# A fused perceiver layer on one core: own-attention links, shift and first expert's chunks issued in another order

## What is computed

```python
x = x + cross_attention(layernorm(x), ctx)   # 16 heads of 16; softmax over 1601 keys
x = x + own_attention(layernorm(x))          # 16 heads of 16, causal, over the batch's 64 rows
x = x + experts(layernorm(x))                # 8 experts 256->1024->256, gelu, best 2 by router
```

## Time and profile before

| | |
|---|---|
| median of 3 runs | 663.91 us (663.18 to 666.14) |
| profiled execution | 663.55 us, its span 661.7 us |
| TensorE busy | 630.8 us, 95% of the span |
| VectorE busy | 475.3 us, 72% |
| ScalarE busy | 329.4 us, 50% |
| GpSimd busy | 301.9 us, 46% |
| TensorE, 400 to 450 us | 45.26 us busy, granted clock 0.97 |
| TensorE, 450 to 500 us | 45.02 us busy, granted clock 0.93 |
| TensorE, 500 to 600 us | 100.00 us busy, granted clock 1.00 |

### The profile page before, as it was taken

One profiled execution on the slowest core, in us unless ns is written; L12 is line 12 of the kernel. 1 busy time (PEld: TensorE's weight loads), 2 busy tenths in 40 slices (PEclk: granted clock), 3 DMA queues, 4 the chain that ended last, 5 costly groups with the idle time before them and its releaser, 6 DMA issues.

```text
span 661.7 us, 15583 instructions
## 1 busy us (share of the span) xinstructions
PE 630.8 (95%) x6304; PEld 532.8 (81%) x6312; DVE 475.3 (72%) x878; ACT 329.4 (50%) x541; POOL 301.9 (46%) x386
## 2 busy tenths in 40 slices
PE   7989999999989989989998999978989999999997
PEld 4778878868877868877887888757879999999997
DVE  4887757667687678688777868686777666656753
ACT  4355655555554555446555545463654444444421
POOL 2138788897686688678678768200000000000000
PEclk9999999999989999999999999998989999999999
DMA  6311110100010010011110000423003302330000
GB/s 184 134 50 52 28 51 26 51 27 26 27 52 1 27 50 27 26 27 51 27 27 26 2 1 2 152 106 127 1 1 128 128 26 104 127 127 0 0 0 33
DMA packets 13285, 34.11 MB, mean 52 GB/s; under 512 B 1563, under 2 KB 10532, under 8 KB 11044
## 3 DMA queue, kind: packets, MB, share of 16 engines
q1 hardware_dynamic: 13188, 33.19, 15.1%
q0 software_dynamic: 32, 0.01, 0.0%
HBM read 32.67 MB, written 0.52 MB: 50 GB/s over the span
## 4 chain that ended last, share of the span: by engine, by line
PE 74%; DVE 13%; issue 5%; ACT 3%; POOL 3%; DMA 2%; SPq 0%; POOLq 0%; DVEq 0%; ACTq 0%
PE bank L1207 46%; PE bank L1396 8%; PE bank L1216 7%; PE bank L1382 4%; PE bank L1277 3%; POOL prob_sum L490 3%; DVE maxes L923 3%; DVE ctx_lo L474 2%; DMA raw<-in_w 1%; ACT k_hi L626 1%; DVE k_lo L904 1%; PE bank L1332 1%; PE bank L1320 1%; PE bank L1304 1%; DVE prob_sum L490 1%
## 5 line engine op out<-in xcount | busy, mean ns | idle before, releaser
L490 POOL TENSOR_TENSOR prob_sum<-probs,prob_sum 128x256 f32<-128x256 f32 x336 | 270.6, 837 | 71.4 <-ACT probs L739 66.4
L739 ACT ACTIVATE probs<-bank 128x1024 f32<-128x1024 f32 (+1 forms) x104 | 106.6, 1025 | 111.6 <-PE bank L1396 99.2
L923 DVE TENSOR_REDUCE maxes<-bank 128x1 f32<-128x400 f32 (+1 forms) x256 | 129.5, 564 | 20.3 <-PE bank L1277 19.8
L721 ACT ACTIVATE h_raw<-bank,b_sb 128x512 f32<-128x512 f32 (+2 forms) x72 | 46.2, 642 | 106.5 <-PE bank L1207 106.3
L904 DVE SCALAR_TENSOR_TENSOR k_lo<-bank,bias_sb,k_hi 128x400 fp32r<-128x400 f32 (+2 forms) x64 | 40.5, 632 | 48.6 <-ACT k_hi L626 48.6
L1207 PE MATMUL bank<-w_hi,h_hi 128*128 128x256 f32 x256 | 73.6, 288 | 0.8 <-DVE h_lo L1142 0.8
L1207 PE MATMUL bank<-w_lo,h_hi 128*128 128x256 f32 x256 | 72.9, 285 | 0.0
L1207 PE MATMUL bank<-w_hi,h_lo 128*128 128x256 f32 x256 | 72.8, 284 | 0.0
L1216 PE MATMUL bank<-probs,v_sb 128*32 128x128 f32 (+1 forms) x1664 | 68.1, 282 | 1.0 <-ACT probs L739 0.5
L1141 DVE CAST h_hi<-h_raw 128x512 fp32r<-128x512 f32 (+2 forms) x72 | 28.5, 396 | 55.5 <-ACT h_raw L721 54.1
L1207 PE MATMUL bank<-wv_hi,ctx_hi 128*128 128x256 f32 (+1 forms) x208 | 65.3, 314 | 2.6 <-DVE maxes L923 2.4
(11 more groups left out here) (155 smaller groups left out, 1389.8 us busy)
## 6 DMA issues: line engine op xcount, KB each, us to landing
raw<-in_w SPq DMA_DIRECT2D x16, 1024.0 KB, 6.8
ctx_raw<-in_ctx_t SPq DMA_DIRECT2D x16, 400.0 KB, 3.6
ctx_raw<-in_ctx_t SPq DMA_DIRECT2D x8, 402.0 KB, 3.8
ctx_raw<-in_ctx_t SPq DMA_DIRECT2D x8, 399.0 KB, 3.6
w_sb<-in_w_t SPq DMA_DIRECT2D x1, 1280.0 KB
w_raw<-in_w_t SPq DMA_DIRECT2D x2, 256.0 KB, 4.7
result<-x_all SPq DMA_DIRECT2D x4, 128.0 KB, 2.0
x_all<-in_x SPq DMA_DIRECT2D x1, 384.0 KB, 4.1
```

What stands on the lines that cost most here:

```text
L490: ins = engine.tensor_tensor(prob_sum[0:ROWS[k], cols], probs[0:ROWS[k], s % 2, cols], acc[0:ROWS[k]], ALU.add)
L721: nc.scalar.activation(h_raw[:, c % 2, 0:width], bank[:, at, 0:width], ACT.Gelu, bias=b1_sb[:, bass.ds(e, 1), c:c + 1].rearrange("p a b -> ...
L739: nc.scalar.activation(probs[0:ROWS[k], s % 2, :].rearrange("p (g n) -> p g n", g=G), bank[0:ROWS[k], score_bank(b, k):score_bank(b, k) + ...
L923: nc.vector.tensor_reduce(maxes[:, g * PAIRS + j, c:c + 1], src[:, 0:width], AX.X, ALU.max).then_inc(read_dve, 1)
```

## The change

Six edits of order; no operation is added, removed or made larger. The table entries of the chain from t10 to the router move one step forward (gt and b2 stay), the second spreading of the own queries stands right behind the first read of the buffer (before the row maxima of s0), `find_shift` stands behind the last step's maxima instead of at the start of the next step (before the context split that used to come between), and the first expert's chunks 0 and 1 go into banks 4 and 5 and stand around the last weighing, before the last denominators; the other chunks follow one place sooner.

```diff
-FIND_SHIFT_AT = KT - 3
+FIND_SHIFT_AT = max(M_AT)
...
-CHAIN_AT = {3: ["y1"], 5: ["xt1"], 6: ["qk", "v"], 8: ["s0"], 10: ["s1"], 12: ["t00", "t01"], 14: ["t10", "t11"],
-            15: ["o0"], 16: ["o1"], 18: ["y2"], 20: ["xt2"], 21: ["router"], 24: ["gt"], 25: ["b2"]}
+CHAIN_AT = {3: ["y1"], 5: ["xt1"], 6: ["qk", "v"], 8: ["s0"], 10: ["s1"], 12: ["t00", "t01"], 13: ["t10", "t11"],
+            14: ["o0"], 15: ["o1"], 17: ["y2"], 19: ["xt2"], 20: ["router"], 24: ["gt"], 25: ["b2"]}
 
 CHAIN_AT_LAST = {2: ["y1"], 4: ["xt1"], 5: ["qk", "v"], 7: ["s0"], 9: ["s1"], 11: ["t00", "t01"],
-                 13: ["t10", "t11"], 15: ["o0", "o1"], 17: ["y2"], 19: ["xt2"], 20: ["router"], 23: ["gt"],
+                 12: ["t10", "t11"], 14: ["o0", "o1"], 16: ["y2"], 18: ["xt2"], 19: ["router"], 23: ["gt"],
                  24: ["b2"]}
...
-FIRST_HIDDEN = {0: [0, 1], 1: [2], 3: [3, 4], 6: [5], 7: [6], 9: [7]}
-FIRST_GELU = {0: [0, 1], 1: [2], 3: [3, 4], 8: [5, 6], 9: [7]}
-FIRST_SPLIT_H = {0: [0, 1], 2: [2], 4: [3], 7: [4], 8: [5], 11: [6], 12: [7]}
-FIRST_OUTPUT = {1: [0], 2: [1], 6: [2, 3], 8: [4], 9: [5], 12: [6, 7]}
+FIRST_HIDDEN = {0: [2], 1: [3], 3: [4], 6: [5], 7: [6], 9: [7]}
+FIRST_GELU = {0: [0, 1], 1: [2], 2: [3], 4: [4], 8: [5, 6], 9: [7]}
+FIRST_SPLIT_H = {0: [0], 1: [1], 2: [2], 3: [3], 4: [4], 8: [5], 11: [6], 12: [7]}
+FIRST_OUTPUT = {1: [0], 2: [1], 3: [2], 6: [3, 4], 9: [5], 12: [6, 7]}
...
+        def first_bank(c):
+
+            return 4 + c if c < 2 else c % 2
...
                     elif kind in ("s0", "s1"):
 
+                        if kind == "s0" and units is not TAIL:
+                            spread_own_queries(1, qbd2)
                         subtract_maxima(int(kind[1]))
...
-                if "s0" in before and units is not TAIL:
-                    spread_own_queries(1, qbd2)
...
+                    for m, kind, u in units.at[s]:
+                        unit(units, m, kind, u, t - 1, b + 1, (bi + 1) % 2)
                     if k == FIND_SHIFT_AT and more > bi:
-                        n = max(n for j in range(s) for n, kind, _ in units.at[j] if kind == "M")
+                        n = max(n for n, kind, _ in units.at[s] if kind == "M")
                         dve.wait_ge(read_dve, units.before[2] + units.counts(n + 1)[2])
                         find_shift()
-                    for m, kind, u in units.at[s]:
-                        unit(units, m, kind, u, t - 1, b + 1, (bi + 1) % 2)
...
-            weigh(B - 1, 1, KT - 1)
-            denominators(B - 1)
...
+            pe.wait_ge(w_split, PIECES)
+            pe.wait_ge(xn2_split, DONE_TILES)
+            pe.wait_ge(read_act, TAIL.before[1])
+            pe.wait_ge(read_dve, TAIL.before[2])
+            hidden(0, 0, first_bank(0), 0, DONE_TILES)
+            weigh(B - 1, 1, KT - 1)
+            hidden(0, 1, first_bank(1), 0, DONE_TILES)
+            denominators(B - 1)
...
                     if c == 0:
+
                         pe.wait_ge(w_split, 2 * PIECES)
+                        pe.wait_ge(h_ready, 2)
                     output(0, c, c, 4, 0, DONE_TILES)
```

More of the change, by code:

```diff
@@ L772, in _ @@
                 for c in FIRST_GELU.get(s, []):
-                    gelu(0, c, c, c % 2, DONE_TILES * P, c >= 2)
+                    gelu(0, c, c, first_bank(c), DONE_TILES * P, c >= 2)
                 if s == SECOND_HI_AT:
@@ L1511, in _ @@
                 for c in FIRST_HIDDEN.get(s, []):
-                    if c == 0:
-                        pe.wait_ge(w_split, PIECES)
-                        pe.wait_ge(xn2_split, DONE_TILES)
-                    if c >= 2:
+                    if c >= 4:
                         pe.wait_ge(h_ready, c - 1)
-                    hidden(0, c, c % 2, 0, DONE_TILES)
+                    hidden(0, c, first_bank(c), 0, DONE_TILES)
                 for c in FIRST_OUTPUT.get(s, []):
```

## The result

Four executions, the profiled one among them, gave 657.35 us as the median of the changed kernel (656.67 to 658.37), against 663.92 us (663.18 to 666.14) before: a ratio of 0.9917, 95% interval 0.9888 to 0.9947. The forecast was 659.9. The ratios are not quotients of the medians (here 0.9901): in the experiments they compare means, without executions that ran clearly slower at a lower granted clock. The profiled execution took 658.37 us (span 656.6), against 663.55 us (span 661.7): 5.2 us less, where the sum said 4.0. On a second chip the same kernel took 658.99 us (656.55 to 661.27, 7 executions) against 662.94 us, 0.9945 (0.9923 to 0.9967): 4.0 us between the medians.

What follows compares the result with a forecast made beforehand. TensorE, busy 95% of the span, was taken as the bound. Terms of -1.6, -3.3, +2.0, +0.6 and -1.7 summed to -4.0 us: 659.55 profiled, 659.9 as median; own range 658.2 to 661.5, wide range 656.3 to 664.0.

Steps and rivals of the forecast that it cites:

- Tile 1, first batch: At s1 and t00: s1 starts sooner, t00 then waits for the quotient; gain 1.6 us.
- Tile 2, first batch: At s1 and t00: the 1.77 us wait at s1 comes back before t00; gain 0.
- Second batches: Tiles 1 and 2: earlier route ends X's wait for the shift; 1.67 us gained per tile, 3.3 in two.
- Tile 3, t00: The shift now precedes the first division, so t00 waits; loss 2.0 us, between 1.7 and 2.2.
- The load and the last weighing: Tile 3: the first expert's weight load starts 1.0 us later relative to the work; loss 0.6 us, bounds 0 and 1.4.
- The tail: Behind the last denominators: y1 1.2 us sooner, xt1 another 0.5; gain 1.7 us, from 1.2 to 3.7.
- the prediction's own sign: Tile 3: no wait at t00, or a relatively earlier last sum, would mean a wrong account and a larger gain.
- Slow stretches behind t00's new gaps: Three tiles: gaps before t00 each drop the clock, 1.7 us apiece; +1.1, or 665.0 us; chance 0.10.
- The gain is taken elsewhere: Tile 1's t00 or banks of steps 22 and 23 take back 1.6 to 2 us; 661.7 us; chance 0.27.
- The new wait before the values of step 23: Second batches, tiles 1 and 2: a bank whose maximum is read late makes about 0.65 us of new wait.
- TensorE is the bound after all: TensorE's waits merely go and tile 3's division comes 1 us late; -8.2, or 655.7 us; chance 0.13.
- The fourth rival: Load lands 1.4 us late, chunks push the last denominators 1.5 us; -1.7, or 662.2; counted within another rival's 0.27.

Runs made afterwards that it cites:

- e3b_spread: Changed kernel with the second spreading of the own queries behind step 9's last maxima but ahead of the shift, tiles 1 and 2: 660.87 us, ratio 0.9988.
- e1_chain: Changed kernel with both tables of chain links as before the change: 659.54 us, ratio 0.9977.
- e11_gsum: Changed kernel with VectorE instead of GpSimd adding step 11's probabilities in the second batches of tiles 1 and 2: 656.98 us, ratio 0.9934.
- e2_shift: Changed kernel with the shift found at the start of step 10 again: 655.90 us, ratio 0.9916.
- e8_load: Changed kernel with the load of the first expert's first weights released one step later: 662.16 us, ratio 0.9999.
- e4_chunks: Changed kernel with the first expert's chunk tables, banks and first chunks' place as before the change: 661.00 us, ratio 0.9994.
- e6_latesplit: Changed kernel with step 9's context split moved behind the first division in tiles 1 and 2: 654.85 us, ratio 0.9891.
- e3_spread: Changed kernel with the second spreading of the own queries at its old line, now behind the shift: 670.31 us, ratio 1.0129.

## Why the prediction was right, and where it was not

**Tile 1, first batch (-1.6; measured -1.41).** The place and the size are right: s1 without a wait, t00 bound by the quotient, a new wait there (1.72 us, forecast 1.3 to 1.7). The reason is wrong. I wrote that TensorE "had 1.74 us to spare" when it reached t00, but it was late because it ran at half clock for 3.4 us, and the stretch "makes no difference". e3b_spread shows the opposite: without it, TensorE arrives just as the quotient is ready, late s1 or not. At full clock this term is 0; the change gained what the stretch cost, and that the next execution has no such stretch was not forecast.

**Tile 2, first batch (0; measured -0.40).** Right in kind: the wait moves to t00 (1.63 us). e3b_spread puts the 0.4 us on the spreading.

**Second batches (-1.67 each; measured -1.82 and -1.79, then +0.74 and +0.70).** Here the sum missed a step. "In tile 0, POOL's queue and the experts nothing that anyone waits for moves" was false for POOL. GpSimd's sums run behind in this batch; while TensorE waited at X, nothing waited for them. With that wait gone the next exponentials wait for them (248.31). e1_chain and e11_gsum give this 0.5 us a tile; the rest, 0.2, stays unexplained.

**Tile 3, t00 (+2.0; measured +0.79, a wait of 0.77).** The mechanism is right, and e2_shift confirms it by taking the wait away. The size is off. The shift took 1.29 us and not 1.54, and the subtraction behind it 0.69 instead of 1.22. The windows of these subtractions (before, then after) differ in GpSimd's column, the last before the clock: it worked beside the first and stood still beside the second.

```profile
404.75:405.97 1.22, 1.22 (x17) 1.08 (x14) 1.22 (x2) 0.30 (x1) 1.22 (x2) 1.00 0.00 0
```

```profile
402.18:402.87 0.69, 0.69 (x16) 0.56 (x19) 0.69 (x2) 0.69 (x2) 0.00 (x0) 1.00 0.00 0
```

In both traces every subtraction and division of this size with GpSimd idle took 0.69 us, and those with GpSimd busy throughout 0.95 to 1.22. I took these durations as fixed. For the shift that is no explanation: GpSimd was busy beside both, and why one took 1.29 us is open. The rest of the difference came from t00's small slack and earlier maxima, which the runs do not separate.

**The load and the last weighing (+0.6; measured -1.25).** The sign was wrong. The issue came later as forecast: 15.24 us behind t00, against 14.29. But it landed within 7.97 us, not 9.04, so the first cut starts 23.21 us behind t00, against 23.33. From there 0.44 us are `xn_lo`, as forecast, and 0.68 lie in the last steps, where the trace before has the half-clock stretch from 445.2, which the forecast had left in. e8_load shows that the load's term was real. How much of the error is the sooner landing is open: with 8.7 us from issue to cut, as in e3b_spread and e4_chunks, the cut would come 0.8 us later.

By the prediction's own sign the account of tile 3 was wrong: from s0 of tile 3 to the last denominators it took 57.28 us before and 56.82 after, where the sum (+2.0 + 0.6) had 2.6 more.

**The tail (-1.7; measured -1.57).** The number is right, y1 -1.12 and xt1 -0.45, but the first is luck. The forecast saw that the two chunks ran at half clock and still counted the 1.2 us as the change's gain. At full clock they would have been out of y1's way in time (e4_chunks), so this term is 0 and only xt1's 0.45 is the order's.

**The rivals.** Slow stretches behind t00's new gaps did not appear in any trace of this study, with gaps of 1.2 to 1.7 us: that rival fell, as far as the profiled executions show. "The gain is taken elsewhere" was half right in the second batches, by GpSimd rather than by banks. The new wait before the values of step 23 was 0.58 us, where 0.65 was forecast. "TensorE is the bound after all" gave 655.7, and 657.35 lies between it and the forecast; but not by its mechanism, since VectorE set t00 in tiles 1 and 2 in place of the waits at s1. Only its smaller loss in tile 3 came true. The fourth rival did not come about: the first cut came 0.12 us sooner behind t00, and the denominators were not pushed back.

**The sum.** Errors of opposite sign nearly cancelled up to t00 of tile 3 (forecast -2.9, measured -3.19), and the load's sign then made the lead larger. How much of it is the change's work can be estimated. Without its stretches the kernel before would start xt2 some 3.2 us sooner than at 483.82 (1.4 at s1, 1.1 on the chunks, and at 445.2 the whole 0.7 of the last steps, which no run isolates), which leaves 2.9 of the lead of 6.08. From xt2 to the span's end traces with full clock have 176.6 us (e2_shift, e3b_spread, e6_latesplit). With the 1.9 us around the span that makes 659.1 us, against 656.6 measured for the changed kernel: 2.5 us. So 2.5 to 2.9 us of work were saved, not the 4.0 forecast. The executions agree: the best of the kernel before, 659.51 us at 0.994, is 3.0 above the changed kernel's best on the same chip and still has half-clock time in it. The rest of the 6.6 us in the first comparison is fewer halved clocks, which the forecast did not contain, and on the second chip that rest was small. So 2.8 us of the forecast's 4.0 (the 1.6 in tile 1 and the 1.2 at y1) were the price of stretches in one execution, and that the median came near the sum is in part luck. The wide range held (656.3 to 664.0); the forecast's own, 658.2 to 661.5, did not hold 657.35, and held the 658.99 of the second chip.

## What to carry to other kernels

When a wait of TensorE moves away, look at who was running behind during it: here GpSimd's sums took back 0.5 us a tile. Before taking a late arrival for slack, or a delay for something an edit can win, ask at what clock the work before it ran: the half clock stood behind two terms of this sum, 2.8 us beside a net 4.0. And a part of a change can be a loss inside a gain: the early shift cost 1.5 to 2 us, and moving one split of 1.5 us behind a division that the transposes wait for gave 3.2 us between the best executions, more than the 2.5 to 2.9 estimated for the whole change.

## What the runs showed of the hardware

The granted clock is not a function of the program alone: with TensorE's rows equal to 0.1 us up to 438.6, one execution kept 1.00 and the other was granted 0.52, half speed (1.2 of 2.4 GHz) nearly throughout, for 6.8 us. Behind waits of 4.12 and 3.43 us, both in e3_spread, the half clock came, the second time 0.7 us before the wait ended; behind the 1.77 us before s1 it came once in the four such waits of two traces (the kernel before and e3b_spread); behind 1.2 to 1.7 us before t00 it came in none. The Trainium skill's page "TensorE: Matmul & The Clock Gate", section "HAM oscillation — how this bites in real kernels", names only clearly longer gaps as costly, and the waits of its example are clearly longer too; e3_spread agrees with it, and the trace of the kernel before, 0.50 behind 1.77 us, contradicts it.

What a half-clock stretch costs depends on who sets the pace behind it: 3.4 us of it cost 1.4 us where t00 follows s1, and 6.8 us cost 2.4 us in the last weighing.

VectorE's subtraction on two inputs of 128x512 took 0.69 us with GpSimd idle and 1.22 us with GpSimd busy throughout, in the same program place. Over all subtractions and divisions of this size in the traces before and after, it was 0.69 us with GpSimd idle, and 0.95 to 1.22 with GpSimd busy throughout.
